# Mixture-of-experts block with linear attention: token rows scattered to expert slots, and expert results added in HBM by accumulating scatters

## What is computed

```python
cap = int(N * K * CF / E)                  # 2048 * 2 * 1.25 / 8 = 640
logits = x @ Wg.T; top_v, top_i = top_k(logits, 2); gates = softmax(top_v)
pos = cumsum(onehot(flat_e), axis=0) - 1   # place of a choice in its expert
keep = pos_f < cap
exp_batches = zeros(E, cap, d).at[flat_e, pos_safe].set(x[tok], mode='drop')
inp, gate = split(einsum('ecd,edf->ecf', exp_batches, W1))
exp_out = einsum('eci,eid->ecd', gelu(inp) * gate, W2)
out = segment_sum(where(keep, gates_f, 0)[:, None] * exp_out[flat_e, pos], tok)
```

## Time and profile before

| | us |
|---|---|
| median of 3 runs | 187.8 |
| lowest, highest | 181.33, 189.93 |
| span of the profiled execution | 156.1 (2323 instructions) |
| mean granted clock of TensorE | 0.920 |

### The profile page before, as it was taken

How to read it: one execution, slowest core, us unless ns; L and a number is a source line. 1 busy time by engine, 2 the same in 40 slices (tenths; PEclk the granted TensorE clock), 3 DMA queues, 4 the chain that set the end, 5 groups by cost and what they waited for, 6 DMA issues and landing times.

```text
span 156.1 us, 2323 instructions
## 1 busy us (share of the span) xinstructions
PE 111.6 (72%) x745; PEld 103.8 (66%) x745; DVE 93.8 (60%) x251; ACT 72.2 (46%) x165; POOL 99.3 (64%) x111
## 2 busy tenths in 40 slices
PE   0029998399978996999999949609989999630000
PEld 0019975288978994999999949609989887620000
DVE  0699989999668838866535322504276565426940
ACT  0457669356659885054645535403243343124600
POOL 7950369934337777777777777777777777305540
PEclk9999999999999999599999999975899999996555
DMA  4999995000002222222121211121111111189540
GB/s 119 269 375 341 337 347 165 0 0 6 0 0 62 43 53 50 49 58 60 44 62 50 57 50 50 50 50 54 51 50 60 58 53 54 35 227 302 153 124 0
DMA packets 20827, 15.49 MB, mean 99 GB/s; under 512 B 2032, under 2 KB 18672, under 8 KB 20816
## 3 DMA queue, kind: packets, MB, share of 16 engines
q1 hardware_dynamic: 17856, 10.49, 22.7%
q0 software_dynamic: 2240, 4.59, 11.6%
q10 hardware_dynamic: 720, 0.27, 0.8%
HBM read 8.85 MB, written 6.49 MB: 98 GB/s over the span
## 4 chain that ended last, share of the span: by engine, by line
POOL 43%; DVE 16%; issue 15%; PE 11%; DMA 8%; ACT 2%; SPq 1%; DVEq 0%; POOLq 0%; ACTq 0%
POOL gathered L459 22%; POOL y_rows L471 21%; PE bank_y L993 4%; DVE xs L838 4%; DMA expo<-y_rows 4%; DMA xs<-in_x 3%; PE bank_a L1075 2%; PE bank_x L986 2%; DVE hid L765 2%; DMA y_rows<-gathered,slot_target 1%; DVE chosen L753 1%; PE bank_x L1046 1%; DVE stats L684 1%; DVE eq L751 1%; DVE xn L697 1%
## 5 line engine op out<-in xcount | busy, mean ns | idle before, releaser
L459 POOL DMA_INDIRECT gathered<-xn_rows,slot_token x35 | 34.3, 980 | 14.8 <-issue 10.4
L471 POOL DMA_INDIRECT y_rows<-gathered,slot_target x35 | 34.0, 972 | 10.7 <-issue 10.7
L940 DVE TENSOR_TENSOR hid<-gelu,bank_h 128x384 f32<-128x384 f32 (+2 forms) x32 | 16.4, 511 | 20.9 <-ACT gelu L645 20.5
L1197 PE MATMUL bank_y<-w_sb,hid 128*128 128x128 f32 x172 | 24.1, 293 | 1.3 <-issue 1.3
L1197 PEld LDWEIGHTS bank_y<-w_sb,hid 128*128 128x128 f32 x172 | 23.3, 210 | 1.5 <-issue 1.4
L645 ACT ACTIVATE gelu<-bank_h 128x384 f32<-128x384 f32 (+2 forms) x32 | 14.6, 458 | 19.8 <-PE bank_h L975 19.8
L973 PE MATMUL bank_h<-xg_hi,w_lo 128*128 128x384 f32 (+1 forms) x56 | 21.0, 375 | 1.3 <-DVE hid L940 0.9
L975 PE MATMUL bank_h<-xg_hi,w_hi 128*128 128x384 f32 (+1 forms) x56 | 17.8, 317 | 0.0
L974 PE MATMUL bank_h<-xg_lo,w_hi 128*128 128x384 f32 (+1 forms) x56 | 17.6, 315 | 0.0
L973 PEld LDWEIGHTS bank_h<-xg_hi,w_lo 128*128 128x128 f32 x56 | 11.1, 199 | 2.1 <-issue 1.3
L986 PE MATMUL bank_x<-ident,xn 128*128 128x128 f32 x16 | 4.4, 428 | 11.0 <-DVE xn L697 9.7
(11 more groups left out here) (151 smaller groups left out, 266.8 us busy)
## 6 DMA issues: line engine op xcount, KB each, us to landing
w_raw<-in_w SPq DMA_DIRECT2D x4, 512.0 KB, 7.8
y_rows<-zeros SPq DMA_DIRECT2D x2, 1024.0 KB, 11.8
expo<-y_rows SPq DMA_DIRECT2D x8, 256.0 KB, 5.3
xs<-in_x SPq DMA_DIRECT2D x4, 256.0 KB, 4.6
xn_rows<-xn SPq DMA_DIRECT2D x4, 256.0 KB, 4.3
out_block<-xs SPq DMA_DIRECT2D x4, 256.0 KB, 2.3
w_sb<-in_w SPq DMA_DIRECT2D x1, 768.0 KB, 10.8
gathered<-xn_rows,slot_token POOLq DMA_INDIRECT x35, 2.7
```

Of the source, the lines that this page charges most:

```text
L459: nc.gpsimd.indirect_dma_start(gathered[:, n, :], None, xn_rows, bass.IndirectOffsetOnAxis(ap=slot_token[:, n:n + 1], axis=0),).then_inc(r ...
L471: nc.gpsimd.indirect_dma_start(y_rows, bass.IndirectOffsetOnAxis(ap=slot_target[:, n:n + 1], axis=0), gathered[:, n, :], None,).then_inc(y ...
L940: nc.vector.tensor_tensor(hid[s % 2][:, c, 0:cols], gelu[i % 2][:, 0:cols], bank_h[2 * c + 1][:, 0:cols], ALU.mult).then_inc(hid_ready, 1)
L1197: ins = nc.tensor.matmul(bank_y[:, j * D:(j + 1) * D], hid[s % 2][:, c, j * P:(j + 1) * P], w2_sb[:, e, c, :], start=(c == 0), stop=(c == ...
```

## The change

- The lists are gone: no one-hot matrices, no list matmuls, no `targets`. Each token row in SBUF (`xa`, 136 floats) holds, behind its 128 values, the token's number, both choices' ranks and both gates. For each choice and tile GpSimd scatters 128 such rows to their slots in HBM (`x_slots`, L399, 32 scatters); a choice without a slot goes to one of 4096 rows behind the slots (`no_slot`). Before, `x_slots` is filled with vacant rows whose token number points behind the last token (L312, 7 transfers of 128 x 5 x 544 bytes).
- SP waits for all 32 scatters and then loads the rows of each expert with one transfer (L326, 7).
- The token number in the loaded row is the index of the result's scatter. `slot_gates` makes the slot's gate on VectorE (L799, L802) and the evacuation scales with it, one activation per tile (L542). The scatter of results adds (`compute_op=ALU.add`) to one of two sums in HBM, even experts' and odd experts' (`y_sums`, L411, 35). A scatter of an expert waits for the adds of the expert two before it.
- The end adds each of the two sums, 4 transfers and 4 additions of 128 x 512 per sum, the sum of experts 2, 4 and 6 (`side` 1) first (L332, L741).
- GpSimd has two subtractions left (L387, L390); ScalarE's halves of the weights (`upper_w1`) and VectorE's (`lower_w1`) are spread over q, k, v and the steps by tables (`W1_IN_QKV`, `W1_IN_STEP`, `LOW_IN_STEP`).
- The two remaining dense steps stand first in `steps`, then the 14 routed ones; all 14 pieces of attention are at the first six places, that is in the first one and a half dense steps (`PIECE_SPOTS = 6`).
- Relu on ScalarE is gone: the bias of queries and keys has 1 added, the exponential subtracts it, and L716 takes min and max.
- The gates are computed before `before_ready`, and of the gate of dense steps only expert 0's column is kept.

```diff
-DENSE_AFTER = (7, 7)
-ATT_FROM = 36
-GATHERS_AHEAD = 5
-KV_LAG = 8
+KV_LAG = 4
+PIECE_SPOTS = 6
+LOW_IN_STEP = {(0, 0): 1, (0, 1): 2, (1, 0): 3, (1, 1): 4, (3, 1): 5, (5, 1): 6, (7, 1): 7}
...
+    steps = all_token_steps[EARLY:] + [(e, j0, nj, r) for r, (e, j0, nj) in enumerate(routed_steps)]
...
+    x_slots = nc.dram_tensor("x_slots", [R * CAP + TOP_K * N, ROW], F32).ap()
+    y_sums = [nc.dram_tensor(f"y_sums{i}", [N + CAP, D], F32).ap() for i in range(2)]
...
+            for r in range(R):
+                sp.dma_start(x_slots_tiles[:, r, :, :], vacant[:, :, :]).then_inc(vacant_stored, 16)
...
+            sp.wait_ge(rows_out, 16 * TOP_K * T)
+            for r in range(R):
+                sp.dma_start(rows[:, r * ST:(r + 1) * ST, :], x_slots_tiles[:, r, :, :]).then_inc(rows_in[r], 16)
+            for i in (1, 0):
+                sp.wait_ge(y_added[i], 16 * ST * len(range(i, R, 2)))
+                for g in range(G):
+                    sp.dma_start(fetched[:, i, g * GROUP:(g + 1) * GROUP, :],
+                                 y_sums_tiles[i][:, g * GROUP:(g + 1) * GROUP, :]).then_inc(fetched_in[i][g], 16)
...
-                    nc.gpsimd.indirect_dma_start(
-                        gathered[:, n, :], None, xn_rows,
-                        bass.IndirectOffsetOnAxis(ap=slot_token[:, n:n + 1], axis=0),
-                    ).then_inc(rows_in[r], 16)
+            pool.wait_ge(vacant_stored, 16 * R)
+            pool.wait_ge(xn_act_ready, G)
+            for k in range(TOP_K):
+                pool.wait_ge(slots_ready, k + 1)
+                for t in range(T):
+                    nc.gpsimd.indirect_dma_start(
+                        x_slots, bass.IndirectOffsetOnAxis(ap=slot_i[:, k, t:t + 1], axis=0), xa[:, t, :], None,
+                    ).then_inc(rows_out, 16)
+            for r in range(R):
+                if r >= 2:
+                    pool.wait_ge(y_added[r % 2], 16 * ST * (r // 2))
+                for i, (j0, nj) in enumerate(PARTS):
+                    pool.wait_ge(y_evac, len(PARTS) * r + i + 1)
+                    for n in range(r * ST + j0, r * ST + j0 + nj):
+                        nc.gpsimd.indirect_dma_start(
+                            y_sums[r % 2],
+                            bass.IndirectOffsetOnAxis(ap=rows[:, n, TOKEN:TOKEN + 1].bitcast(I32), axis=0),
+                            rows[:, n, 0:D], None, compute_op=ALU.add,
+                        ).then_inc(y_added[r % 2], 16)
...
+                    ins = nc.scalar.activation(rows[:, n, 0:D], bank_y[:, j * D:(j + 1) * D], ACT.Copy,
+                                               scale=gate_slot[:, n:n + 1])
...
+            for k in range(TOP_K):
+                link(nc.vector.tensor_tensor(picked[:, k, :, :], chosen[:, k, :, :], slot_all[:, :, :], ALU.mult))
+                link(nc.vector.tensor_reduce(slot[:, k, :], picked[:, k, :, :], AX.X, ALU.add))
+                nc.vector.tensor_tensor(slot_i[:, k, :], slot[:, k, :], no_slot[:, k, :], ALU.min).then_inc(slots_ready, 1)
...
-            ins.then_inc(slots_ready, 1)
...
+            for side in (1, 0):
+                for g in range(G):
+                    add_fetched(side, g)
```

More of the change, by code:

```diff
@@ L94, in moe_attention_block @@
                       + ([("projection", u - 2)] if u >= 2 else []))
-    hurried = [s for s in range(1, S) if steps[s - 1][3] is not None and steps[s][3] is None][-1]
     spots = [(s, c, i) for s in range(S) for c in range(FC) for i in range(2)]
-    chunks = [(s, c) for s in range(S) for c in range(FC)]
     pieces_at = {}
[L100 to L103, removed]
+    for i, piece in enumerate(pieces):
+        pieces_at.setdefault(spots[i * PIECE_SPOTS // len(pieces)], []).extend(piece)
     sum_tiles, sums_with = [], {}
@@ L110, in note_sum @@
         sums_with[name] = len(sum_tiles)
[L112 to L120, removed]
+    for i in range(EARLY):
+        for j in range(GROUP):
+            note_sum(("early", i), (all_token_steps[i][1] + j,))
+    for s in range(S):
+        for c in range(FC):
+            for i in range(2):
+                for kind, u in pieces_at.get((s, c, i), []):
+                    if kind == "projection":
+                        note_sum((kind, u), (2 * u, 2 * u + 1))
+        if s >= 1 and steps[s - 1][3] is None:
             for j in range(GROUP):
                 note_sum(("step", s - 1), (steps[s - 1][1] + j,))
[L123 to L132, removed]
+    for side in (1, 0):
+        for g in range(G):
+            note_sum(("routed", side, g), tuple(range(g * GROUP, (g + 1) * GROUP)))
     def earlier_sum(index, tiles):
@@ L202, in moe_attention_block @@
         gate_sum = sb("gate_sum", [P, T])
[L203 to L204 removed]
+        gate0 = sb("gate0", [P, T])
         assigned = sb("assigned", [P, T, E], BF16)
[L206 removed]
+        kept = sb("kept", [P, T])
         slot_all = sb("slot_all", [P, T, E])
@@ L1199, in down @@
                 ins.then_inc(down_done, 1)
-            transpose_slots(0)
-            for t in range(T - KV_LAG, T):
-                kv_tile(t)
             pe.wait_ge(val_ready, T)
@@ L1206, in _ @@
                 up(s)
-                if s >= 1 and s != hurried:
+                if s >= 1:
                     down(s - 1)
             down(S - 1)
-            for piece in pieces_at.get("end", []):
-                attention_piece(*piece)
 def kernel(L0_attn_x, L0_attn_gamma, L0_attn_beta, L0_attn_Wqkv, L0_attn_Wout, L0_ffn_Wg, L0_ffn_W1, L0_ffn_W2):
```

518 lines of the change are left out of this document (189 added, 329 removed).

## The result

The changed kernel takes 205.13 us (median of four runs, 205.03 to 205.8) beside 188.87 us for the kernel before (four runs, 181.33 to 193.38): ratio 1.134, 95% interval 1.129 to 1.140. It is slower; 181 us, faster, was forecast.

A forecast was written before the change was run, and what follows sets the result against it. No engine is full; one GpSimd queue of 70 indirect DMAs makes most of the span. Last add landed 137.8 + 5.0 + 0.7 + 5.9 = 149.4 us, plus 31.7 around the span = 181 us, 3.6% below; range 174 to 198 us.

The forecast's parts named there:

- The price of the addition: 35 adding scatters L411: pitch 1.34 us taken, between bounds 1.27 and 2.51; last start 134.9 us.
- Rival A: Adding scatters cost half an instruction more: pitch 1.76 us, span 164, total 196 us; chance 0.24.
- The level: Around the span: median 187.8 us less profiled span 156.1, 31.7 us, taken as constant and added to the forecast span.
- Start of the queue: Token-row scatters L399: first at 30.1 us instead of 44.97, 32 at pitch 1.27, last at 69.5 us.
- Key-value tiles: Tiles of queries, keys and values: VectorE sets the pace, 1.6 us a pair, 8 pairs, end at 52 us.
- Attention in a chain and the restart: Attention pieces serial at 2.0 us each; slot transposes of the first routed step wait for attention until 77.5 us.
- From there to the first result: First routed step, slot transposes to first scatter-add: 11.9 us, so first L411 at 89.3 us.
- Tail: After the last scatter: landing 2.9 us, at 137.8, then fetches 5.0, add 0.7 and 5.9 to the end, 149.4 us.
- B: TensorE at half clock during serial attention, 55 to 78 us: up to 7 us more, total 188 us; chance 0.15.
- C: Token rows land late, each of 32 scatters 0.48 us longer: rows at 90.6 us, total 194 us; chance 0.05.
- D: Attention overlaps better, so rows bind at 75.2 us, and the add is free: total 176 us; chance 0.09.
- The rule that the prediction takes from the Trainium skill: Adding DMAs move at about half rate: doubled transfer still fits the pitch, last landing grows by under half a microsecond.

The follow-up runs named there:

- e5: The changed kernel, nothing edited, on a chip of the low level: 173.95 us against 158.57 us for the kernel before on that chip.
- e3: The changed kernel with GpSimd holding back the 32 scatters of token rows until all queries and keys are done: 194.8 us.
- e7: The changed kernel with the 35 result scatters (L411) plain, without the addition in HBM, so the sum is left out: 151.8 us.
- e11: The changed kernel, complete, with results scattered without adding to y_rows, row token + 2048 x choice: 156.94 us against 158.55 for the kernel before.
- e4: The changed kernel with L710 as a scale and an added 1.0, without the bias tensor of queries and keys: 174.28 us.
- e10: The changed kernel whose 35 result scatters add only the first 64 of the 128 columns of each row: 174.3 us.

## Why the prediction was wrong, step by step

Each step against e5, whose span of 172.9 us is 23.5 us over the forecast 149.4. The chain of e5 in its last part, in order of time:

```profile
157.87 1.55 POOL y_sums L411
159.42 0.30 issue
159.72 3.70 DMA y_sums<-rows
...
164.94 4.21 DMA expo<-y_sums
169.15 0.02 issue
169.18 0.69 DVE xs L741
```

- **The price of the addition: the step that failed.** "I take 1.34, near the row of the same form": the pitch, from one start to the next, was 1.86, with 1.55 of instruction instead of about 1.04. 34 x (1.858 - 1.34) = 17.6 of the 23.5 us. The bounds of 1.27 and 2.51 held it, and the break-even of 1.54 and the 2% point of 1.65 were right in kind; the value taken inside them was not. I placed it beside the plain scatter because the form was the same. The list and the source are the same, and the instruction still took 0.59 us more. Rival A, half an instruction more (1.76), came nearest: its span of 164 us is the closest to 172.9 of all named, still 9 short. Its reason, a third address, is not shown, nor is any other.
- **The level.** The difference between a span and a median of other executions, 31.7 us, was taken as time around a span. It is 1.7 us. This added 30 us to the forecast: without it the forecast would have been 151 against 158, and the measured value 174. That 181 came within 24 us of the measured 205.13 is luck: the changed kernel's span at the high level, 204.1, happens to be 31.2 us over e5's, about what had been added for another reason. The stated range of 174 to 198 us holds neither 205.13 nor, quite, 173.95.
- **Start of the queue.** Forecast 30.1 us for the first L399, measured 28.9; last forecast at 69.5, measured 70.3. Right at both ends, but partly by luck: the pitch was (70.3 - 28.9) / 31 = 1.34 instead of 1.27, and the early start made up for it. Most scatters took 0.96 us, as assumed; a few took 1.2 to 1.6.
- **Key-value tiles.** Forecast end 52, measured 57.3 (e5). "VectorE then sets the pace", 1.6 us a pair: it took 2.2 (from the first L710 at 38.0 us to the sixteenth at 54.5). It was not the scatters, as e3 shows. L710 waits 0.9 us for TensorE before 8 of its 16 runs, and TensorE's L952 waits 14 times for VectorE's L716 (8.6 us in e5): the two answer each other in turn, where I had VectorE alone.
- **Attention in a chain and the restart.** Pieces at 2.0 us: measured 2.06 (bank_a L989 at 74.33, 76.40, 78.46). From the key-value end to the slot transposes 26.5 us, forecast 25.5. They wait for the sums of attention (L760), as forecast, not for rows: e5's transposes begin at 83.8 us, forecast 77.5; the 6.3 are 5.3 from the step above and 1.0 from here. The row of the transposes:

```profile
83.81 0.52 PE L1019 MATMUL bank_x<-ident,rows 128*128 128x128 f32 x3 [0.60 <-DVE xs L760]
```

- **From there to the first result.** 11.8 us forecast, 12.7 measured; first L411 at 96.5, forecast 89.3. No wait for y_added, as forecast.
- **Tail.** Landing 2.9 forecast, 3.7 measured (from the start of the instruction, which is itself 0.6 longer); from there 11.6 forecast, 9.5 measured.

Sum: +17.6 for the pitch, +7.2 for the start, +0.8 and -2.1 for the tail are 23.5. Without the error in the pitch the step errors would have given a span of 149.4 + 7.2 + 0.8 - 2.1 = 155.3 us, under the 156.1 of before, and e7, which has the plain pitch, ran in spans of 149.1 to 152.0. The account of everything but the addition was right in sign; the addition decided the whole.

Of the rivals, B (clock at half) did not come at the low level: e5's granted clock is 1.00 from 40 to 60, from 55 to 90 and from 100 to 130 us. C (late rows) did not come by itself, and e3 shows its price, 20 us for row loads issued 25 us later. D fails on both its terms: attention bound the restart, and the addition was not free.

The rule that the prediction takes from the Trainium skill (Collectives: The Full Stack, "The bandwidth ceiling: the fold count and why AG ≠ RS ≠ AR") is stated there for ring collectives, where a reduce reads two sources and gets about half the rate of a copy; that it holds for one accumulating DMA was the prediction's own step. What the runs show: the median from the start of a scatter to its landing was 3.3 us with the addition (e5, 100 to 140 us) and 2.2 without (e7, 100 to 136), and 0.6 of the 1.1 is the longer instruction. The last landings alone are 3.70 in e5 and 3.32 in e7, 0.4 apart. And the transfers stayed under the pitch (40% of the DMA engines). So the remainder of about half a microsecond fits that use of the rule, and the 20 us went where it does not look, to the engine that issues.

## What to carry to other kernels

An operation that the trace does not show, and that repeats 35 times on the path, can decide the forecast: its price has to be spread over its bounds in the chances, not set beside the nearest look-alike. If results are summed by indirect scatters that GpSimd issues back to back, count 1.86 us for an adding one and 1.26 for a plain one; two plain targets and additions on VectorE at the end (0.69 us for 128x512) were cheaper here, where GpSimd's queue is the path: e11 has 156.94 us, e5 173.95. A number from one execution and a median of others must first be shown to be of the same level, by a control on one chip, before the difference is given a meaning; e4 without e5 would have "proved" a mechanism that does not exist here.

## What was not expected of the hardware

An accumulating indirect DMA of 128 rows costs GpSimd 1.55 us instead of 0.96, whether it moves 512 or 256 bytes a row and in both kernels. In the records the DMA engines get it in more pieces. The changed kernel has 6064 packets in the software queue; the page of e7, the same kernel without the addition, has

```profile
DMA packets 29083, 19.90 MB, mean 131 GB/s; under 512 B 2144, under 2 KB 26976, under 8 KB 29072
...
q0 software_dynamic: 2144, 4.53, 8.7%
```

and the page of the changed kernel sorts its packets by size so:

```profile
DMA packets 33003, 19.90 MB, mean 98 GB/s; under 512 B 2144, under 2 KB 31456, under 8 KB 32992
```

From 512 B to 2 KB there are 31456 - 26976 = 4480 packets more, which is 35 x 128: one for each added row. From 2 to 8 KB there are (29072 - 26976) - (32992 - 31456) = 560 fewer, which is 35 x 16: a plain scatter moves its 128 rows in 16 packets, as many as there are DMA engines. The packets of less than 512 B are as many in both kernels; in e10, whose added rows have 256 B, they are 6624 instead of 2144, again 4480 more. Whether GpSimd's 0.59 us has to do with these pieces is not shown.

And the level: three chips ran the kernels at one level (157 to 160 and 173 to 175 us), one at another (193 and 205), with waits on TensorE, ScalarE and VectorE that no releaser explains.
